# A two-layer perceiver kernel: products of the weights' low 64 rows in pairs on the two halves of the array

## The chip, the core and the metric

The kernel runs on one core of one Trainium2 chip. The metric is the device time of one execution in microseconds (us). A core has five engines with queues of their own: TensorE (PE in the profile; its weight loads are PEld), VectorE (DVE), ScalarE (ACT), GpSimd (POOL) and SyncE (SP), which issues the DMAs. They meet only at semaphores: a wait at the head of an engine's queue holds back all that stands behind it.

## What is computed

Six blocks are added to a residual `x` of 128 tokens x 256. The change touches two, the cross attentions over a context of 12544 rows x 192:

```python
x = x + _L0_xattn_ref(_layernorm(x), ctx_768, ...)   # 16 heads of 16
...
x = x + _L1_xattn_ref(_layernorm(x), ctx_768, ...)   # 16 heads of 64
# in each:
q = x @ Wq;  k = context @ Wk;  v = context @ Wv      # context 12544 x 192
sim = jnp.einsum('bhid,bhjd->bhij', q, k) * SCALE
attn = jax.nn.softmax(sim, axis=-1)
out = jnp.einsum('bhij,bhjd->bhid', attn, v)
```

Between and behind them stand a self attention, two mixtures of eight experts and one more attention over `x` itself; nothing in them is changed.

## The kernel before

Precision beyond float16 comes from splitting: a number is kept as a float16 (hi) and the float16 of what is left (low), and a product is summed from several float16 products in PSUM. The 192 rows of the context's transpose do not fit the 128 rows of the array. The first 128 lie in `ctxT_a_hi` and `ctxT_a_lo`. The last 64 lie in `ctxT_b`: its partitions 0 to 63 hold their hi part, 64 to 127 their low part. The weights stand in four parts, `wk16` and `wv16`: part 0 (first 128 rows, hi), part 1 (first 128 rows, low), part 2 (last 64 rows, hi, twice, so that one product covers hi x hi and low x hi) and part 3 (last 64 rows, low; its upper 64 partitions are zero). A key or value sum is therefore five products, all with 128 rows; in the fifth half of the rows are zeros.

The context has 98 tiles of 128 tokens (NT), in 14 chunks (NCH) of 7 tiles (CH, 896 columns). Each cross attention has two passes.

- The first pass (`first_pass`, L761) works by a list of turns written out beforehand, `TURNS`. PE transposes the chunks (layer 0 alone; `turn_ab` L697, `turn_lo` L709), makes key blocks of 128 rows x 896 columns in two PSUM banks of 448 (`project_keys` L715), and multiplies them with the queries (`score_pair` L749) to find each query's maximum. `score_pair` works with 64 rows: its two heads stand in the two halves of the array. ACT copies a block's hi part out (`keys_out` L1078, recorded at L1090 or L1088), DVE takes the low part (`keys_low_out` L1282, recorded at L1261 or L1291), and SP stores both to DRAM. Half of the maxima are reduced by DVE (L1324), the others copied by ACT (L1102) and merged by DVE (`merge`, L1261). Layer 0 has 28 blocks, layer 1 has 112. Layer 0's values are also made there (`values0` L740).
- The second pass of layer 1 (`attend1` L870) runs over two halves `g` of 8 heads, each over 98 tiles. PE's order in an iteration `t` is: five products for the values of tile `t` (`value_products` L733, 512 columns each), 16 score products (`score1` L835), and 16 products that weigh the values of tile `t - 1` (`weigh1` L853). ACT (L1143) takes the exponential of each group of four heads twice, once as float16 and once in place, and in odd tiles copies the values' hi part (L1156) ahead of that. DVE (L1407) first makes the values of tile `t` (`split_values1` L1362: in even tiles a cast, L1369, and a subtraction; in odd tiles only the subtraction), and then the low parts of the two groups of probabilities (L1261). The values have two PSUM banks in turn (`v_bank` L352), so the products of tile `i` wait until the values of `i - 2` are made (`values_made`, L879). Keys come back chunk by chunk (`load_keys1` L451), which may start once the chunk two before has been scored.

Nearly all matmuls are recorded at L679, a helper; they are told apart by their tiles.

Of the kernel before, what the change touches and what calls it, by code (L numbers as in the profile page):

```python
# [7 lines left out]
F32 = mybir.dt.float32  # L8
# [5 lines left out]
P = 128  # L14
# [27 lines left out]
def perceiver_kernel(nc, d, out):  # L42
# [18 lines left out]
    with ExitStack() as ctx:  # L61
# [39 lines left out]
        minus_half = sb("minus_half", [P, 1], F32)  # L101
        ps = ctx.enter_context(nc.psum_tensor("ps", [P, 8, 512], F32))
        col_in = att[:, 0:P]
        bk_scaled = small[:, 234:236]
# [67 lines left out]
        L0.wq, L0.wk, L0.wv = W[:, 0:512], W[:, 512:1024], W[:, 1024:1536]  # L172
        L0.wk16 = wv16[:, :, 256:512]
        L0.running = W[:, 5568:9152].bitcast(F16).rearrange("p (h k) -> p h k", h=H // 2)
        L0.k_parts = [W[:, 9152 + 448 * n:9152 + 448 * (n + 1)].bitcast(F16) for n in range(6)]
# [25 lines left out]
        QUERIES = (1, 2)  # L201
        W1_OFF, W2_OFF, CA_OFF = 7616, 8640, 9664

        def wview(off, a, b):
# [355 lines left out]
        def gpsimd(pool):  # L560
# [6 lines left out]

            def split_weights16(w, dst, n):
                top, rest = w[:, 0:n], w[0:CB, n:2 * n]
                settle(pool.tensor_scalar(top, top, VS, None, ALU.mult))  # L570
                settle(pool.tensor_copy(dst[:, 0, :], top))
                settle(pool.tensor_tensor(dst[:, 1, :], top, dst[:, 0, :], ALU.subtract))
                settle(pool.tensor_scalar(rest, rest, VS, None, ALU.mult))
                settle(pool.tensor_copy(dst[0:CB, 2, :], rest))
                settle(pool.tensor_tensor(dst[0:CB, 3, :], rest, dst[0:CB, 2, :], ALU.subtract))
                return pool.tensor_copy(dst[CB:P, 2, :], rest)

# [15 lines left out]
            pool.wait_ge(constants, 1)  # L593
            pool.memset(wv16[CB:P, 3, :].bitcast(F32), 0.0).then_inc(rows_blank, 1)
            pool.wait_ge(rows_blank, 1)
# [5 lines left out]
            pool.wait_ge(ld_w, PROJ_IN[0])  # L601
            split_weights16(L0.wk, L0.wk16, 256).then_inc(wk_made, 1)
            pool.wait_ge(wk_made, 1)
# [16 lines left out]
            pool.wait_ge(ld_wv, WV_IN[0])  # L620
            settle(split_weights16(L0.wv, wv16[:, :, 0:256], 256))
            settle(pool.memset(v_out[:, 0:VROW], 0.0))
# [19 lines left out]
            pool.wait_ge(step_pe, PE_B2)  # L642
            settle(pool.memset(L1.wk16[CB:P, 3, :].bitcast(F32), 0.0))
            pool.memset(q_two[CB:P, :].bitcast(F32), 0.0).then_inc(rows_blank, 1)
# [18 lines left out]
            pool.wait_ge(ld_wv, WV_IN[1])  # L663
            settle(split_weights16(L1.wv, wv16[:, :, 0:1024], 1024))
            for n in range(2):
# [11 lines left out]
        def tensor(pe):  # L677
# [19 lines left out]
            def turn_ab(c, slot):  # L697
                c16 = ctx16[c % 4]
                hi, b = (ps[:, 2 * slot + n, :].bitcast(F16) for n in range(2))
                pe.wait_ge(ctx_split, c + 1)  # L700
                for t in range(CH):
                    pe.transpose(hi[:, t * P:(t + 1) * P], c16[:, t, 0:P], ident16[:, :])
                for t in range(CH):
                    s = slice(t * P, (t + 1) * P)
                    pe.transpose(b[0:CB, s], c16[:, t, P:C], ident16[:, :])
                    ins = pe.transpose(b[CB:P, s], c16[:, t, C + P:2 * C], ident16[:, :])
                ins.then_inc(ab_turned, 1)
# [7 lines left out]
            def project_keys(L, b, slot):  # L715
                c, i = b // L.nI, b % L.nI
                ws = slice(i * P, (i + 1) * P)
                pe.wait_ge(wk_made, L.n + 1)
                if L is L0 and i == 0:
                    pe.wait_ge(hi_out, c + 1)  # L720
                    pe.wait_ge(b_out, c + 1)
                    pe.wait_ge(lo_out, c + 1)
                for n in range(MAXB):
                    ks = slice(c * CLEN + n * MAXC, c * CLEN + (n + 1) * MAXC)
                    o = ps[:, 2 * slot + n, 0:MAXC]
                    mm(o, L.wk16[:, 0, ws], ctxT_a_hi[:, ks], True, False)
                    mm(o, L.wk16[:, 1, ws], ctxT_a_hi[:, ks], False, False)
                    mm(o, L.wk16[:, 0, ws], ctxT_a_lo[:, ks], False, False)
                    mm(o, L.wk16[:, 2, ws], ctxT_b[:, ks], False, False)
                    ins = mm(o, L.wk16[:, 3, ws], ctxT_b[:, ks], False, True)  # L730
                ins.then_inc(keys_summed, 1)

            def value_products(o, ks, vs):  # L733
                mm(o, ctxT_a_hi[:, ks], wv16[:, 0, vs], True, False)
                mm(o, ctxT_a_hi[:, ks], wv16[:, 1, vs], False, False)
                mm(o, ctxT_a_lo[:, ks], wv16[:, 0, vs], False, False)
                mm(o, ctxT_b[:, ks], wv16[:, 2, vs], False, False)
                return mm(o, ctxT_b[:, ks], wv16[:, 3, vs], False, True)

            def values0(c, u, slot):  # L740
                pe.wait_ge(wv_made, 1)
                a, b = VPARTS[u]
                for t in range(a, b):
                    k = c * CH + t
                    ins = value_products(ps[:, 2 * slot, (t - a) * L0.gw:(t - a + 1) * L0.gw],
                                         slice(k * P, (k + 1) * P), slice(0, L0.gw))
                ins.then_inc(values0_summed, 1)
# [87 lines left out]
            def score1(g, t, j):  # L835
                i, n = (g * NT + t) * 2 + j, g * NCH + t // CH
                if i >= 3:
                    pe.wait_ge(low_made, i - 2)
                if t % CH == 0 and j == 0:
                    pe.wait_ge(ld_keys[n % 2], 48 * (NCH // 2) + 48 * (n // 2 + 1))  # L840
                    if n == 1:
                        pe.wait_ge(keys_const, 3)
                own = slice(t % CH * P, (t % CH + 1) * P)
                both, hi = KW1[n % 2]
                for k in range(4):
                    hh = 4 * j + k
                    qs = slice((8 * g + hh) * P, (8 * g + hh + 1) * P)
                    o = s_bank(i)[:, k * P:(k + 1) * P]
                    mm(o, both[:, hh, own], q_one[:, qs], True, False)
                    ins = mm(o, hi[:, hh, own], q_two[:, qs], False, True)  # L850
                ins.then_inc(scored, 1)

            def weigh1(g, t):  # L853
# [14 lines left out]
                ins.then_inc(weighed, 1)  # L868

            def attend1():  # L870
                first_pass(L1)
                pe.wait_ge(wv_made, 2)
                pe.wait_ge(keys_const, 2)
                for g in range(2):
                    for t in range(NT + 1):
                        if t < NT:
                            i = g * NT + t
                            if i >= 2:
                                pe.wait_ge(values_made, i - 1)  # L879
                            value_products(v_bank(i), slice(t * P, (t + 1) * P),  # L880
                                           slice(g * L1.gw, (g + 1) * L1.gw)).then_inc(values_summed, 1)
                            if g == 0 and t == 0:
                                pe.wait_ge(q_placed, 2)
                                pe.wait_ge(rows_made, 2)
                            for j in range(2):
                                score1(g, t, j)
                        if t:
                            weigh1(g, t - 1)
# [174 lines left out]
        def scalar(act):  # L1063
# [14 lines left out]
            def keys_out(L, b, slot):  # L1078
                n = L.k0 + b
                src = ps[:, 2 * slot:2 * slot + 2, 0:MAXC]  # L1080
                dst = k_part(L, b, 0).rearrange("p (n k) -> p n k", n=MAXB)
                act.wait_ge(keys_summed, n + 1)
# [169 lines left out]
        def vector(dve):  # L1252
# [29 lines left out]
            def keys_low_out(L, b, slot):  # L1282
                n = L.k0 + b
                src = ps[:, 2 * slot:2 * slot + 2, 0:MAXC]
                hi, low = (k_part(L, b, part).rearrange("p (n k) -> p n k", n=MAXB) for part in range(2))
                dve.wait_ge(keys_hi, n + 1)
# [226 lines left out]
            for e in range(NE):  # L1513
# [8 lines left out]
                                     op0=ALU.mult, op1=ALU.subtract)  # L1522
            dve.scalar_tensor_tensor(out=L1.wk16[0:CB, 3, :], in0=wk_b, scalar=VS, in1=L1.wk16[0:CB, 2, :],
                                     op0=ALU.mult, op1=ALU.subtract).then_inc(wk_made, 1)
            dve.wait_ge(q_hi, 4)
# [76 lines left out]
```

## Time and profile before

| | us |
|---|---|
| median of three runs (1548.43 to 1552.89) | 1550.3 |
| the profiled execution | 1556.26 |
| its span, first to last instruction | 1554.5 |

| engine | busy us | share of the span |
|---|---|---|
| PE | 1396.2 | 90% |
| PEld | 925.5 | 60% |
| DVE | 1055.4 | 68% |
| ACT | 1062.3 | 68% |
| POOL | 89.9 | 6% |

The chain that ended last is 60% PE and 21% DVE, 11% is issue and 4% DMA. The stages, by the profile's slices: layer 0's first pass until about 280 us, its second pass to 488, the small blocks and layer 0's experts to 613, layer 1's first pass from 622 to about 909, its second pass from about 919 to 1477, the rest to the end. A busy share says how full an engine was, not whether the others waited for it; ends of matmuls are modelled, so the distance between two starts is the safer number.

### The profile page before, as it was taken

The page shows a single profiled execution, that of the slowest core. Times are in us where ns is not written, and L with a number is a line of the kernel's source. Part 1 is how long each engine was busy: PE and PEld are TensorE (multiplying, and loading weights), DVE is VectorE, ACT ScalarE, POOL GpSimd, SP SyncE. Part 2 cuts the span into 40 slices and gives each one's busy share as a digit, 9 for nine tenths or more (in the row PEclk, how much of TensorE's full clock was granted, in tenths as well). Part 3 has the DMA queues.
Part 4 walks back from the last instruction along what each step waited for, and adds up shares of the span by engine and source line. Part 5 has one row for each costly group of instructions (what it writes and reads, how often), then busy time and mean ns, then how long its engine had stood idle before and what let it go on. Part 6 is the DMA issues. An engine that isn't in the chain of part 4 may idle for free.

```text
span 1554.5 us, 36882 instructions
## 1 busy us (share of the span) xinstructions
PE 1396.2 (90%) x15312; PEld 925.5 (60%) x15312; DVE 1055.4 (68%) x1480; ACT 1062.3 (68%) x1628; POOL 89.9 (6%) x85
## 2 busy tenths in 40 slices
PE   4888888799998789999999959999998999989959
PEld 2334444576775578343443427777776777767748
DVE  4899999200001311899999978888888888878832
ACT  3677777698995023666666648888887888878810
POOL 5311111000000001400000000000000000000000
PEclk9999999999998689999999979999999999999969
DMA  4245433775765134554454487777777677796620
GB/s 133 107 143 211 150 120 141 197 175 142 177 158 191 54 112 153 207 185 183 178 187 181 180 194 138 149 147 148 149 139 140 118 148 148 149 259 117 175 98 4
DMA packets 128458, 236.47 MB, mean 152 GB/s; under 512 B 8908, under 2 KB 113830, under 8 KB 128294
## 3 DMA queue, kind: packets, MB, share of 16 engines
q1 hardware_dynamic: 128294, 234.13, 57.0%
q8 instruction: 122, 2.00, 0.6%
q14 instruction: 42, 0.34, 0.1%
HBM read 155.98 MB, written 78.12 MB: 151 GB/s over the span
## 4 chain that ended last, share of the span: by engine, by line
PE 60%; DVE 21%; issue 11%; DMA 4%; ACT 2%; SPq 2%; POOL 0%; POOLq 0%; DVEq 0%; ACTq 0%
PE ps L679 59%; DVE W L1261 6%; DVE p L1261 5%; DVE small L1324 5%; DMA W<-keys_hi 2%; SPq L402 1%; DMA W<-in_ctx_dram 1%; ACT W L1088 1%; DVE W L1291 1%; DVE q_all L1261 1%; SPq L460 0%; ACT p L1102 0%; DVE ctxT_a_lo L1317 0%; DMA att<-in_L_ffn_b_dram 0%; DVE ctxT_b L1313 0%
## 5 line engine op out<-in xcount | busy, mean ns | idle before, releaser
L1261 DVE TENSOR_TENSOR p<-ps,p 128x512 f16<-128x512 f32 (+1 forms) x467 | 353.0, 756 | 76.5 <-ACT ps L1065 74.1
L1065 ACT ACTIVATE p<-ps 128x512 f16<-128x512 f32 (+1 forms) x490 | 329.3, 682 | 99.3 <-PE ps L679 97.0
L679 PE MATMUL ps<-q_all,W 128*128 128x128 f16 (+2 forms) x3544 | 264.3, 227 | 15.6 <-DMA W<-keys_hi 11.0
L679 PEld LDWEIGHTS ps<-q_all,W 128*128 128x128 f16 (+1 forms) x3544 | 230.8, 99 | 77.2 <-issue 25.5
L1324 DVE TENSOR_REDUCE small<-ps 128x1 f32<-128x896 f32 x224 | 245.3, 1096 | 6.1 <-PE ps L679 5.8
L1065 ACT ACTIVATE ps<-ps 128x512 f32<-128x512 f32 x392 | 236.0, 602 | 0.0
L679 PE MATMUL ps<-v,p 128*128 128x130 f16 x3136 | 170.4, 207 | 5.4 <-DVE p L1261 3.8
L679 PE MATMUL ps<-wv,ctxT_a_hi 128*128 128x512 f16 (+1 forms) x588 | 156.3, 347 | 13.6 <-DVE W L1291 6.1
L679 PE MATMUL ps<-wv,ctxT_b 128*128 128x512 f16 (+1 forms) x588 | 155.5, 346 | 0.0
L679 PEld LDWEIGHTS ps<-v,p 128*128 128x128 f16 x3136 | 148.4, 98 | 11.7 <-ACT ps L1065 4.0
L1261 DVE TENSOR_TENSOR v<-ps,v 128x512 f16<-128x512 f32 x196 | 135.5, 691 | 17.4 <-ACT v L1156 4.9
L1377 DVE COPY att<-ps 128x512 f32<-128x512 f32 x1 | 0.7, 690 | 207.5 <-PE ps L679 207.5
L679 PE MATMUL ps<-W,q_all 64*128 64x448 f16 (+1 forms) x684 | 105.7, 365 | 29.2 <-DVE ctxT_a_lo L1317 9.4
L679 PE MATMUL ps<-ctxT_a_hi,q_all 128*128 128x448 f16 (+1 forms) x464 | 126.3, 356 | 0.6 <-DVE p L1261 0.6
L679 PE MATMUL ps<-ctxT_b,q_all 128*128 128x448 f16 (+1 forms) x464 | 125.1, 353 | 0.0
L1090 ACT CAST p<-ps 128x896 f16<-128x896 f32 x75 | 67.9, 905 | 61.0 <-PE ps L679 60.9
L1102 ACT CAST p<-ps 128x896 f16<-128x896 f32 x104 | 92.8, 906 | 18.4 <-PE ps L679 17.6
L679 PE MATMUL ps<-wv,ctxT_a_lo 128*128 128x512 f16 (+1 forms) x294 | 102.0, 347 | 0.0
L1065 ACT ACTIVATE W<-ps 128x1024 f32<-128x1024 f32 x98 | 95.0, 1021 | 8.6 <-PE ps L679 6.4
L679 PEld LDWEIGHTS ps<-wv,ctxT_b 128*128 128x128 f16 x588 | 57.9, 99 | 49.7 <-issue 2.2
L679 PEld LDWEIGHTS ps<-W,q_all 64*128 64x128 f16 (+1 forms) x684 | 35.7, 108 | 81.9 <-issue 38.8
L679 PE MATMUL ps<-ctxT_a_lo,q_all 128*128 128x448 f16 (+1 forms) x240 | 82.7, 354 | 0.0
(223 smaller groups left out, 1753.5 us busy)
## 6 DMA issues: line engine op xcount, KB each, us to landing
W<-keys_hi SPq DMA_DIRECT2D x56, 896.0 KB, 14.7
W<-keys_low SPq DMA_DIRECT2D x28, 896.0 KB, 11.7
keys_hi<-p SPq DMA_DIRECT2D x75, 224.0 KB, 2.0
keys_low<-p SPq DMA_DIRECT2D x75, 224.0 KB, 1.9
keys_hi<-W SPq DMA_DIRECT2D x65, 224.0 KB, 2.0
keys_low<-W SPq DMA_DIRECT2D x65, 224.0 KB, 1.9
W<-values SPq DMA_DIRECT2D x14, 960.0 KB, 9.2
W<-in_L_ffn_W_dram SPq DMA_DIRECT2D x10, 1024.0 KB, 8.9
```

The lines of the kernel that those rows point to most:

```text
L402: sp.dma_start(by_rows(region, a, n), src.rearrange("(a p) n -> p a n", p=P)).then_inc(s, 16)
L679: return pe.matmul(out_, lhsT, rhs, start=start, stop=stop, **kw)
L1065: return act.activation(out_, in_, ACT.Exp, scale=scale)
L1088: ins = act.activation(dst, src, ACT.Identity, bias=bk_scaled[:, i:i + 1])
L1090: ins = act.copy(dst, src)
L1102: act.copy(dst.rearrange("p (n k) -> p n k", n=MAXB), src).then_inc(max_copied, 1)
L1261: return dve.tensor_tensor(out_, a, b, op)
L1291: ins = dve.scalar_tensor_tensor(out=low, in0=src, scalar=bk_scaled[:, i:i + 1], in1=hi, op0=ALU.add, op1=ALU.subtract)
L1324: dve.tensor_reduce(mpart[:, among(L, h), n:n + 1], ps[:, 2 * pair:2 * pair + 2, 0:MAXC], AX.XY, ALU.max).then_inc(max_reduced, 1)
L1377: dve.tensor_copy(att[:, 512:1024], ps[:, O0_BANK, :]).then_inc(outT_made, 1)
```

## The change

Part 3 of the weights (the low part of the last 64 rows) is written to both halves of the partitions instead of one half and zeros. `ctxT_b` is laid out in two ways: `half_of(c, t)` says in which half of the partitions a tile's hi part lies; tiles 0 to 3 of a chunk differ from tiles 4 to 6, and even chunks from odd ones. So the fifth product can be made with 64 rows, in one half of the array or the other, by the tile.

```diff
+        FIRST = 4
+        def half_of(c, t):
+            return (t >= FIRST) ^ c % 2
+        def tile_at(i):
+            c, r = i // CH, i % CH
+            return c * CH + (r // 2 if r % 2 == 0 else FIRST + r // 2)
...  turn_ab
+                    k = half_of(c, t)
+                    pe.transpose(b[k * CB:(k + 1) * CB, s], c16[:, t, P:C], ident16[:, :])
+                    ins = pe.transpose(b[(1 - k) * CB:(2 - k) * CB, s], c16[:, t, C + P:2 * C], ident16[:, :])
...  project_keys: banks of 512 and 384 columns; four products each as before, then
+                for n, (k0, k1) in enumerate(banks):
+                    k = half_of(c, FIRST * n)
+                    rows = slice(k * CB, (k + 1) * CB)
+                    ins = mm(ps[:, 2 * slot + n, 0:k1 - k0], L.wk16[rows, 3, ws],
+                             ctxT_b[rows, c * CLEN + k0:c * CLEN + k1], False, True)
...  layer 1's values
+            def values1(i):
+                g, t = i // NT, tile_at(i % NT)
+                vs = slice(g * L1.gw, (g + 1) * L1.gw)
+                if i >= 2:
+                    pe.wait_ge(values_made, i - 1)
+                value_products(v_bank(i), slice(t * P, (t + 1) * P), vs)
+                if i % 2:
+                    for n, t in ((i - 1, tile_at(i % NT - 1)), (i, t)):
+                        k = half_of(t // CH, t % CH)
+                        rows = slice(k * CB, (k + 1) * CB)
+                        mm(v_bank(n), ctxT_b[rows, t * P:(t + 1) * P], wv16[rows, 3, vs], False, True).then_inc(values_summed, 1)
...  attend1, in iteration t
-                            if i >= 2:
-                                pe.wait_ge(values_made, i - 1)
-                            value_products(v_bank(i), slice(t * P, (t + 1) * P),
-                                           slice(g * L1.gw, (g + 1) * L1.gw)).then_inc(values_summed, 1)
+                            if t == 0:
+                                values1(i)
+                            if i + 1 < 2 * NT and t + 1 < NT:
+                                values1(i + 1)
```

`value_products` is now the first four products. In layer 1's second pass the tiles of a chunk are taken in the order 0, 4, 1, 5, 2, 6, 3 (`tile_at`), so that halves alternate; `score1` takes the same order. Layer 0's values keep five products of 128 rows: their part 3 exists in two forms, with the zeros below or above, and the tile chooses. The keys' copies out of PSUM read 896 columns in one run instead of 2 x 448. POOL's `split_weights16` ends with one more copy of 64 rows; for layer 1's keys DVE makes part 3 in two instructions (L1523), and POOL's memset of its zeros (L643) goes.

## Rows read from the trace of the kernel before

**Rows 1.** Three stretches: busy us of PE, PEld, DVE, ACT, POOL, then clock, DMA.

```profile
120.00:200.00 80.00, 63.98 (x534) 33.21 (x532) 76.83 (x91) 58.29 (x73) 13.76 (x5) 1.00 0.47 169
760.00:800.00 40.00, 40.00 (x224) 15.89 (x222) 40.00 (x49) 26.94 (x33) 0.00 (x0) 1.00 0.49 180
1000.00:1100.00 100.00, 99.83 (x1369) 77.10 (x1367) 85.58 (x130) 85.90 (x167) 0.00 (x0) 1.00 0.75 145
```

**Rows 2.** Timeline, layer 1's first pass: start, duration, engine, line, out<-in, count [idle].

```profile
761.61 1.11 DVE L1324 TENSOR_REDUCE small<-ps 128x1 f32<-128x896 f32 x1
762.61 1.11 DVE L1261 TENSOR_TENSOR p<-ps,p 128x896 f16<-128x896 f32 x1
763.61 0.64 DVE L1261 TENSOR_TENSOR W<-W,att 128x896 f16<-128x896 f16 x1
763.77 0.11 PEld L679 LDWEIGHTS ps<-ctxT_a_hi,q_all 128*128 128x128 f16 x2 [0.42 <-DVE p L1261]
764.14 1.11 DVE L1324 TENSOR_REDUCE small<-ps 128x1 f32<-128x896 f32 x1
```

**Rows 3.** Timeline, the same pass in its first chunk, PE alone.

```profile
629.28 0.54 PE L679 MATMUL ps<-ctxT_b,q_all 128*128 128x448 f16 x2
629.75 0.55 PE L679 MATMUL ps<-W,q_all 64*128 64x448 f16 x4
630.24 0.55 PE L679 MATMUL ps<-ctxT_a_hi,q_all 128*128 128x448 f16 x2
...
632.72 0.55 PE L679 MATMUL ps<-ctxT_a_hi,q_all 128*128 128x448 f16 x2
```

**Rows 4.** Timeline, layer 0's first pass, VectorE.

```profile
188.64 0.61 DVE L1261 TENSOR_TENSOR W<-W,p 128x896 f16<-128x896 f16 x1
189.39 1.15 DVE L1291 SCALAR_TENSOR_TENSOR W<-ps,small,W 128x896 f16<-128x896 f32 x1
```

**Rows 5.** Timeline, layer 1's second pass, two tiles: even from 1061.54, odd from 1064.29.

```profile
1061.54 0.59 PE L679 MATMUL ps<-wv,ctxT_a_hi 128*128 128x512 f16 x2
1061.97 0.38 PE L679 MATMUL ps<-wv,ctxT_a_lo 128*128 128x512 f16 x1
...
1062.62 1.06 PE L679 MATMUL ps<-q_all,W 128*128 128x128 f16 x16
...
1063.26 0.60 ACT L1065 ACTIVATE p<-ps 128x512 f16<-128x512 f32 x1 [0.54 <-PE ps L679]
...
1064.29 0.59 PE L679 MATMUL ps<-wv,ctxT_a_hi 128*128 128x512 f16 x2
...
1065.37 1.06 PE L679 MATMUL ps<-q_all,W 128*128 128x128 f16 x16
1065.57 0.59 ACT L1156 CAST v<-ps 128x512 f16<-128x512 f32 x1 [0.21 <-PE ps L679]
1066.05 0.60 ACT L1065 ACTIVATE p<-ps 128x512 f16<-128x512 f32 x1
...
1066.95 0.59 PE L679 MATMUL ps<-wv,ctxT_a_hi 128*128 128x512 f16 x2
...
1068.17 0.69 DVE L1261 TENSOR_TENSOR p<-ps,p 128x512 f16<-128x512 f32 x1 [0.30 <-ACT ps L1065]
...
1068.78 0.68 DVE L1369 CAST v<-ps 128x512 f16<-128x512 f32 x1
...
1069.49 0.69 DVE L1261 TENSOR_TENSOR v<-ps,v 128x512 f16<-128x512 f32 x1
```

**Rows 6.** Waits of PE from 925 to 1485: total us, times, longest.

```profile
PE ps L679 <- DMA W<-keys_hi: 11.0, 2, 6.0
...
PE ps L679 <- issue: 3.5, 6, 1.4
```

**Rows 7.** Timeline, where the low parts of the keys' weights are made.

```profile
23.18 0.39 POOL L576 CAST wv<-W 64x256 f16<-64x256 f32 x1
...
616.54 1.21 DVE L1523 SCALAR_TENSOR_TENSOR q_all<-stage,q_all 64x1024 f16<-64x1024 f32 x1
```

More of the change, by code:

```diff
@@ L102, in perceiver_kernel @@
         ps = ctx.enter_context(nc.psum_tensor("ps", [P, 8, 512], F32))
+        ps_row = ps[:, :, :].rearrange("p b n -> p (b n)")
         col_in = att[:, 0:P]
@@ L173, in perceiver_kernel @@
         L0.wk16 = wv16[:, :, 256:512]
+        L0.wv_low = wv16[:, 3, 0:256], wv16[:, 3, 512:768]
         L0.running = W[:, 5568:9152].bitcast(F16).rearrange("p (h k) -> p h k", h=H // 2)
@@ L566, in rsqrt_var, with split_weights16 @@
                 pool.tensor_tensor(rstd, rstd, minus_half[:, :], ALU.pow).then_inc(ln_rstd, 1)
-            def split_weights16(w, dst, n):
+            def split_weights16(w, dst, n, low):
                 top, rest = w[:, 0:n], w[0:CB, n:2 * n]
@@ L575, in split_weights16 @@
                 settle(pool.tensor_tensor(dst[0:CB, 3, :], rest, dst[0:CB, 2, :], ALU.subtract))
-                return pool.tensor_copy(dst[CB:P, 2, :], rest)
+                pool.tensor_copy(dst[CB:P, 2, :], rest)
+                return pool.tensor_copy(low, dst[0:CB, 3, :])
             pool.memset(ident[:, :], 0.0)
@@ L593, in gpsimd @@
             pool.wait_ge(constants, 1)
-            pool.memset(wv16[CB:P, 3, :].bitcast(F32), 0.0).then_inc(rows_blank, 1)
+            pool.memset(wv16[CB:P, 3, 0:256].bitcast(F32), 0.0)
+            pool.memset(wv16[0:CB, 3, 512:768].bitcast(F32), 0.0).then_inc(rows_blank, 1)
             pool.wait_ge(rows_blank, 1)
@@ L601, in gpsimd @@
             pool.wait_ge(ld_w, PROJ_IN[0])
-            split_weights16(L0.wk, L0.wk16, 256).then_inc(wk_made, 1)
+            split_weights16(L0.wk, L0.wk16, 256, L0.wk16[CB:P, 3, :]).then_inc(wk_made, 1)
             pool.wait_ge(wk_made, 1)
@@ L620, in gpsimd @@
             pool.wait_ge(ld_wv, WV_IN[0])
-            settle(split_weights16(L0.wv, wv16[:, :, 0:256], 256))
+            settle(split_weights16(L0.wv, wv16[:, :, 0:256], 256, L0.wv_low[1][CB:P, :]))
             settle(pool.memset(v_out[:, 0:VROW], 0.0))
@@ L642, in gpsimd @@
             pool.wait_ge(step_pe, PE_B2)
-            settle(pool.memset(L1.wk16[CB:P, 3, :].bitcast(F32), 0.0))
             pool.memset(q_two[CB:P, :].bitcast(F32), 0.0).then_inc(rows_blank, 1)
@@ L663, in gpsimd @@
             pool.wait_ge(ld_wv, WV_IN[1])
-            settle(split_weights16(L1.wv, wv16[:, :, 0:1024], 1024))
+            settle(split_weights16(L1.wv, wv16[:, :, 0:1024], 1024, wv16[CB:P, 3, 0:1024]))
             for n in range(2):
@@ L704, in turn_ab @@
                     s = slice(t * P, (t + 1) * P)
-                    pe.transpose(b[0:CB, s], c16[:, t, P:C], ident16[:, :])
-                    ins = pe.transpose(b[CB:P, s], c16[:, t, C + P:2 * C], ident16[:, :])
+                    k = half_of(c, t)
+                    pe.transpose(b[k * CB:(k + 1) * CB, s], c16[:, t, P:C], ident16[:, :])
+                    ins = pe.transpose(b[(1 - k) * CB:(2 - k) * CB, s], c16[:, t, C + P:2 * C], ident16[:, :])
                 ins.then_inc(ab_turned, 1)
@@ L722, in project_keys @@
                     pe.wait_ge(lo_out, c + 1)
-                for n in range(MAXB):
-                    ks = slice(c * CLEN + n * MAXC, c * CLEN + (n + 1) * MAXC)
-                    o = ps[:, 2 * slot + n, 0:MAXC]
+                banks = ((0, FIRST * P), (FIRST * P, CLEN))
+                for n, (k0, k1) in enumerate(banks):
+                    ks = slice(c * CLEN + k0, c * CLEN + k1)
+                    o = ps[:, 2 * slot + n, 0:k1 - k0]
                     mm(o, L.wk16[:, 0, ws], ctxT_a_hi[:, ks], True, False)
@@ L729, in project_keys @@
                     mm(o, L.wk16[:, 2, ws], ctxT_b[:, ks], False, False)
-                    ins = mm(o, L.wk16[:, 3, ws], ctxT_b[:, ks], False, True)
+                for n, (k0, k1) in enumerate(banks):
+                    k = half_of(c, FIRST * n)
+                    rows = slice(k * CB, (k + 1) * CB)
+                    ins = mm(ps[:, 2 * slot + n, 0:k1 - k0], L.wk16[rows, 3, ws],
+                             ctxT_b[rows, c * CLEN + k0:c * CLEN + k1], False, True)
                 ins.then_inc(keys_summed, 1)
@@ L737, in value_products @@
                 mm(o, ctxT_b[:, ks], wv16[:, 2, vs], False, False)
-                return mm(o, ctxT_b[:, ks], wv16[:, 3, vs], False, True)
             def values0(c, u, slot):
@@ L744, in values0 @@
                     k = c * CH + t
-                    ins = value_products(ps[:, 2 * slot, (t - a) * L0.gw:(t - a + 1) * L0.gw],
-                                         slice(k * P, (k + 1) * P), slice(0, L0.gw))
+                    o, ks = ps[:, 2 * slot, (t - a) * L0.gw:(t - a + 1) * L0.gw], slice(k * P, (k + 1) * P)
+                    value_products(o, ks, slice(0, L0.gw))
+                    ins = mm(o, ctxT_b[:, ks], L0.wv_low[half_of(c, t)], False, True)
                 ins.then_inc(values0_summed, 1)
@@ L842, in score1 @@
                         pe.wait_ge(keys_const, 3)
+                t = tile_at(t)
                 own = slice(t % CH * P, (t % CH + 1) * P)
@@ L1079, in keys_out @@
                 n = L.k0 + b
-                src = ps[:, 2 * slot:2 * slot + 2, 0:MAXC]
-                dst = k_part(L, b, 0).rearrange("p (n k) -> p n k", n=MAXB)
+                src, dst = ps_row[:, 1024 * slot:1024 * slot + CLEN], k_part(L, b, 0)
                 act.wait_ge(keys_summed, n + 1)
@@ L1283, in keys_low_out @@
                 n = L.k0 + b
-                src = ps[:, 2 * slot:2 * slot + 2, 0:MAXC]
-                hi, low = (k_part(L, b, part).rearrange("p (n k) -> p n k", n=MAXB) for part in range(2))
+                src = ps_row[:, 1024 * slot:1024 * slot + CLEN]
+                hi, low = (k_part(L, b, part) for part in range(2))
                 dve.wait_ge(keys_hi, n + 1)
@@ L1522, in vector @@
                                      op0=ALU.mult, op1=ALU.subtract)
-            dve.scalar_tensor_tensor(out=L1.wk16[0:CB, 3, :], in0=wk_b, scalar=VS, in1=L1.wk16[0:CB, 2, :],
-                                     op0=ALU.mult, op1=ALU.subtract).then_inc(wk_made, 1)
+            for k in range(2):
+                ins = dve.scalar_tensor_tensor(out=L1.wk16[k * CB:(k + 1) * CB, 3, :], in0=wk_b, scalar=VS,
+                                               in1=L1.wk16[0:CB, 2, :], op0=ALU.mult, op1=ALU.subtract)
+            ins.then_inc(wk_made, 1)
             dve.wait_ge(q_hi, 4)
```

## The prediction, made before the changed kernel was run

> **What bounds the kernel now.** I read the stretches of each stage first, then the timelines inside them. In both first passes VectorE is the full engine: 76.83 of 80 us in layer 0, 40.00 of 40 in layer 1, at full TensorE clock (1.00, the 2.4 GHz level) [rows 1]. Inside layer 1 the order is reduce, subtraction, merge, reduce, each starting as the one before drains: starts at 761.61, 762.61, 763.61, 764.14, so 2.53 us a block, all of it VectorE [rows 2]. In layer 1's second pass PE is the full engine (99.83 of 100 us, DVE 85.58, ACT 85.90) [rows 1]. There two tiles take 1066.95 - 1061.54 = 5.41 us of PE starts without a gap: five value products of 0.215 each (two in 1061.97 - 1061.54 = 0.43) make 1.08, scores and weighing 1.67 in the even tile and 1.58 in the odd [rows 5]. So only PE work of that last stage is on the path that sets the end, and of the change only what falls there can count in full.
>
> **The change, part by part.** The sum is made against the profiled execution, 1556.3 us, which is 6.0 above the median of 1550.3; I take the difference over to the median.
>
> *Keys.* A block loses two fifth products of 448 columns (2 x 0.19: 629.66 less 629.28 is the pace [rows 3]) and gains a pair in two halves that lasts as long as its longer one, 512 columns, 0.215. That is 0.16 us of PE per block. That such pairs overlap the trace shows: the four 64-row products of 448 columns start at 629.75 and the next product starts at 630.24, 0.49 later, where four in a row would take 0.76 [rows 3]. In layer 1, 104 of 112 blocks run at VectorE's 2.53 [rows 2]: gain 0. In its first chunk there is nothing to merge and PE sets the pace, 632.72 - 630.24 = 2.48 a block [rows 3], while VectorE has two operations of 1.0: 8 x 0.16 = -1.3. In layer 0 VectorE waits only for the block that follows its queue's merge: 189.39 - 188.64 = 0.75, where that step takes 0.53 elsewhere [rows 2, 4]. Of this 0.22, 0.16 goes, in some 13 chunks: -2. Bounds: 0 and 28 x 0.16 = -4.5.
>
> *Weights.* POOL's extra copy of 64 x 256 costs about 0.39 [rows 7] ahead of the first keys, of which the queries' placing hides most: I take +0.4. DVE's second L1523 (1.21 [rows 7]) lies beside the query projection of layer 1, for whose end both engines wait: 0. The other copies on POOL lie beside 250 us of first pass, and the transposes are as many as before: 0. If the cover of these were gone it would be +0.4, +1.2 and, for 64 x 1024 on POOL, a few us.
>
> *Layer 1's values, PE's side.* Per two tiles one product of 512 columns goes: -0.215, or -21 us over 98 pairs, if PE still sets the pace and nothing else is added.
>
> *Layer 1's values, the waits.* This is where I part from the plain sum. The even tile's last product is now issued with the odd tile's, at the same place in PE's order as before (1.08 us into the even iteration). But its successor's place has moved: the products of tile t + 2 now stand at the head of iteration t + 1, one whole iteration earlier, and they need the bank that tile t's split still reads (`values_made`). Before, the split had 5.41 - 1.08 = 4.3 us; now it has scores and weighing of one iteration, 1.67 us. It does not fit: it is a cast and a subtraction, and in VectorE's queue it stands behind the last low part of the tile before. The rows show it: low part at 1068.17, cast at 1068.78, subtraction at 1069.49 to 1070.18, while the even iteration began at 1066.95: the values are made 3.23 us into it, and the next iteration's products would want them after 2.6 to 2.75 [rows 5].
>
> That closes a loop, which I follow from the start of an odd iteration (four products, of the even tile to come):
> - four products 4 x 0.215 = 0.86;
> - scores start to first exponential: 1063.26 - 1062.62 = 0.64 (the even tile, where ScalarE was idle; the odd tile's copy, which held ScalarE up at 1065.57, can now go before the scores, as its values are summed an iteration earlier);
> - first exponential to the last low part of that tile: 1068.17 - 1066.05 = 2.12;
> - low part to cast 0.61, cast to subtraction 0.71, subtraction 0.69;
> - its end to PE's next weight load: 763.77 - (762.61 + 1.11) = 0.05 [rows 2].
>
> The sum is 5.68 (0.86 + 0.64 + 2.12 + 0.61 + 0.71 + 0.69 + 0.05), and with 0.01 for a cold start of the first product 5.69, against 5.41 now. PE's own work in the pair of tiles is 5.20, so it would stand for about 0.5 us before every even tile's products. Behind that wait stand the odd tile's scores, so ScalarE and VectorE come late too, which is why the loop doesn't close shorter. The odd tile's values (copy on ScalarE, subtraction) are made 1.9 us into the odd iteration and are wanted at 2.45: no wait. Per pair +0.28, 98 pairs: +27.4. At each half's start two tiles' products are issued ahead of the first scores, beside a wait, and the last iteration has none: -0.9 twice, -2 in all.
>
> *The keys' loads.* PE waits 11.0 us for keys in this stage, 6.0 of them at its start, and 3.5 for "issue", mostly at a new chunk's first scores [rows 6]. The loads run beside the tiles; a chunk of seven tiles will take 19.9 instead of 18.9 us, and the 5 us wait that remains comes two chunks after its loads may start. Back come 3 of the 3.5, and 2 of the 5: -5. Bounds: 0 and -8.5.
>
> *A rule on the array's modes.* Value products have 128 rows on both sides of the new pair. Before the change such a change of rows happens between keys and scores: the second 448-column product of [rows 3] ends at 629.66 and the 64-row ones start at 629.75; they last 0.38 and the next 128-row product starts at 630.24: 0.09 and 0.11 us beyond the streams. So a pair among the values costs about 0.2 on top, in the even iteration, where PE otherwise stands 0.5: the loop is unchanged, and my sum too. In the keys the number of changes stays two a block. The Trainium skill ("TensorEngine Tiling (Array Packing)", Tiling Modes, Key Properties) says that changing the tiling mode drains TensorE, and that speaks against this change: by it PE's side would gain nothing even without the new wait; without it PE's side would give -21.
>
> The sum: +27.4 - 2 - 5 - 2 - 1.3 + 0.4 = +17.5. Profiled 1573.8, median **1567.8 us**.
>
> **The rivals.**
> - *The wait is not late, and PE keeps the pace; changes of rows are free.* 98 x -0.215 = -21, -3.3 from the first passes, and about +4 as chunks of 18.2 us run into the keys' loads (three issue waits would each grow by 0.7, and more appear): 1530. For it: PE is at 99.83%. Against it: the loop would have to be 0.3 to 0.5 us shorter than rows of this very sequence.
> - *PE keeps the pace, and the changes of rows cost what rows 3 show.* -21 + 98 x 0.2 - 3 = -4: 1546 to 1550, no change to barely faster. It needs the same shorter loop, below 5.4.
> - *The pairs do not overlap.* Then the even iteration has 0.2 more, still under the 0.5 for which PE stands (with the changes of rows just under it), and the first passes give nothing: 1571. Against it: the 0.49 us for four in [rows 3].
> - *The clock.* PE stands still every 5.7 us; if that brought the granted clock to the 1.2 GHz level for stretches, each pair of tiles there would take some 4 us more, hundreds of us if all through. Against it: in layer 0's first pass PE is busy 63.98 of 80 us, in bits, and the clock is 1.00 [rows 1]; here it would be 91%.
>
> **How the numbers follow.** Forecast 0.80; no overlap 0.06; clock 0.02 (slower by far); PE keeps the pace with the costs of a row change 0.06 (half of it beyond the bound of faster), free 0.05; 0.01 left. About what can be told from no change is 0.3%, 4.7 us. The range: each 0.05 us in the loop is 5 us; with 0.1 either way it is -10 and +10; the loads add from +5 (nothing back) to -3.5, the first passes +3 to -2.5. Put together these give 1556 to 1580, which with the no-overlap case holds about 0.85. Faster 0.08, same 0.04, slower 0.88.
>
> **What would show it.** In layer 1's second pass: two tiles in 5.69 us; PE's waits before `ctxT_a_hi` products on `DVE v`, one in each two tiles, 0.3 to 0.5 us, 30 to 45 us in sum, or on PEld; low part, cast and subtraction back to back on VectorE; VectorE and ScalarE less busy than before. In layer 1's first pass still 2.53 us a block, with longer idle on PE. Layer 0's first pass 2 us shorter. Wrong it would be if two tiles take 5.4 or less: then the split's place in VectorE's queue or the exponentials' start is not as I put it. If they take 5.69 and the total is still below 1560, my loads' share was too small.

## The result

| | median us | against before, 95% interval |
|---|---|---|
| before | 1551.4 (4 runs) | |
| changed | 1574.96 (1573.3 to 1582.01, 4 runs) | 1.0163 [1.0127, 1.0199] |
| changed, once more | 1574.79 (6 runs; before 1552.23, 11 runs) | 1.0144 [1.0122, 1.0165] |

The change makes the kernel slower by 1.4% to 1.6%, 22 to 25 us. The forecast was 1567.8, slower, so the direction came true and the size was 5 to 7 us too small. The profiled execution of the changed kernel took 1573.87 us with a span of 1572.1, 17.6 above the profiled one of before, which was 5 us above its own median.

### The profile page after: what moved, and what is told of

It reads as the page before. It is cut to its first block, busy times and chain, and to the rows that moved or that the text cites. A ratio compares the mean times of both kernels' runs of the same rounds, so it can differ in the third digit from the quotient of the medians.

```text
span 1572.1 us, 36886 instructions
## 1 busy us (share of the span) xinstructions
PE 1381.3 (88%) x15312; PEld 899.4 (57%) x15312; DVE 1047.6 (67%) x1481; ACT 1064.6 (68%) x1628; POOL 90.8 (6%) x88
## 4 chain that ended last, share of the span: by engine, by line
PE 38%; DVE 25%; issue 20%; ACT 9%; DMA 4%; SPq 2%; POOL 0%; POOLq 0%; DVEq 0%; ACTq 0%
PE ps L695 37%; ACT ps L1101 6%; DVE p L1296 5%; DVE W L1296 5%; DVE small L1359 4%; DVE v L1296 4%; DVE v L1404 4%; DMA W<-keys_hi 2%; SPq L417 1%; DMA W<-in_ctx_dram 1%; ACT W L1123 1%; DVE W L1326 1%; ACT p L1101 1%; DVE q_all L1296 1%; DMA keys_hi<-p 0%
## 5 line engine op out<-in xcount | busy, mean ns | idle before, releaser
L695 PEld LDWEIGHTS ps<-q_all,W 128*128 128x128 f16 (+1 forms) x3544 | 222.9, 99 | 69.5 <-issue 41.7
L1359 DVE TENSOR_REDUCE small<-ps 128x1 f32<-128x896 f32 x224 | 241.7, 1080 | 4.1 <-PE ps L695 3.8
L695 PE MATMUL ps<-wv,ctxT_b 128*128 128x256 f16 (+2 forms) x588 | 144.7, 349 | 0.0
L695 PE MATMUL ps<-ctxT_a_hi,q_all 128*128 128x512 f16 (+1 forms) x464 | 126.3, 356 | 15.2 <-DVE p L1296 0.6
L695 PE MATMUL ps<-ctxT_b,q_all 128*128 128x512 f16 (+1 forms) x464 | 118.5, 357 | 0.0
L695 PEld LDWEIGHTS ps<-ctxT_a_hi,q_all 128*128 128x128 f16 (+1 forms) x464 | 37.6, 101 | 89.8 <-DVE p L1296 41.9
L695 PEld LDWEIGHTS ps<-wv,ctxT_b 128*128 128x128 f16 (+1 forms) x588 | 48.0, 96 | 68.0 <-issue 43.1
L695 PE MATMUL ps<-ctxT_a_lo,q_all 128*128 128x512 f16 (+1 forms) x240 | 82.7, 354 | 0.0
```

The source lines that it names most:

```text
L695: return pe.matmul(out_, lhsT, rhs, start=start, stop=stop, **kw)
L1359: dve.tensor_reduce(mpart[:, among(L, h), n:n + 1], ps[:, 2 * pair:2 * pair + 2, 0:MAXC], AX.XY, ALU.max).then_inc(max_reduced, 1)
```

## The profile after

First the same three stretches as in [rows 1]. In layer 1's first pass VectorE is full as before and PE falls from 40.00 to 37.65; in the second pass PE falls from 99.83 to 96.42, VectorE from 85.58 to 79.55 and ScalarE from 85.90 to 82.38, at the same full clock. All three are less busy in the second pass, as they are when each waits for another in turn.

```profile
120.00:200.00 80.00, 63.24 (x524) 32.55 (x526) 77.83 (x93) 59.65 (x76) 13.67 (x5) 1.00 0.44 158
760.00:800.00 40.00, 37.65 (x223) 15.13 (x222) 40.00 (x48) 26.91 (x33) 0.00 (x0) 1.00 0.50 184
1000.00:1100.00 100.00, 96.42 (x1297) 70.17 (x1296) 79.55 (x123) 82.38 (x160) 0.00 (x0) 1.00 0.73 139
```

Next the timeline of two tiles of the changed kernel's second pass, the answer to [rows 5]. The even iteration begins at 1059.85, the odd one at 1063.10, the next even one at 1065.56: 5.71 us for two tiles (1065.56 - 1059.85), against 5.41.

```profile
1059.85 0.59 PE L695 MATMUL ps<-wv,ctxT_a_hi 128*128 128x512 f16 x2
...
1060.50 0.70 PE L695 MATMUL ps<-wv,ctxT_b 128*128 128x512 f16 x3
1060.81 0.10 PEld L695 LDWEIGHTS ps<-wv,ctxT_b 64*128 64x128 f16 x2 [0.42 <-issue]
...
1061.03 0.69 DVE L1296 TENSOR_TENSOR p<-ps,p 128x512 f16<-128x512 f32 x1 [0.31 <-ACT ps L1101]
...
1061.13 1.07 PE L695 MATMUL ps<-q_all,W 128*128 128x128 f16 x16
1061.63 0.68 DVE L1404 CAST v<-ps 128x512 f16<-128x512 f32 x1
...
1062.35 0.69 DVE L1296 TENSOR_TENSOR v<-ps,v 128x512 f16<-128x512 f32 x1
...
1063.09 0.11 PEld L695 LDWEIGHTS ps<-wv,ctxT_a_hi 128*128 128x128 f16 x2 [0.35 <-DVE v L1296]
1063.10 0.60 PE L695 MATMUL ps<-wv,ctxT_a_hi 128*128 128x512 f16 x2 [0.20 <-DVE v L1296]
...
1063.97 1.06 PE L695 MATMUL ps<-q_all,W 128*128 128x128 f16 x16
...
1064.62 0.60 ACT L1101 ACTIVATE p<-ps 128x512 f16<-128x512 f32 x1 [0.23 <-PE ps L695]
...
1065.56 0.59 PE L695 MATMUL ps<-wv,ctxT_a_hi 128*128 128x512 f16 x2
...
1066.74 0.69 DVE L1296 TENSOR_TENSOR p<-ps,p 128x512 f16<-128x512 f32 x1 [0.31 <-ACT ps L1101]
```

On VectorE the low part (1061.03), the cast (1061.63) and the subtraction (1062.35 to 1063.04) stand behind each other; PE's next weight load starts at 1063.09, 0.05 after it, behind the wait. From PE's start at 1063.10: scores after 0.87, exponential after 0.65, low part after 2.12, and around again.

The chain of waits over such a stretch (start, duration, what) runs through just these links; in the kernel before, the same view of this stage named only PE.

```profile
1063.10 1.50 PE ps L695 x12
...
1065.11 0.59 ACT ps L1101
...
1066.10 0.61 ACT ps L1101
...
1066.74 0.04 DVE p L1296
...
1067.34 0.69 DVE v L1404
1068.06 0.70 DVE v L1296
1068.76 0.05 issue
1068.81 1.50 PE ps L695 x12
```

PE's waits in this stage (columns as in [rows 6], but from 915 to 1500, since the stage begins 7 us earlier here): the new one comes 86 times in the matmuls' record. The loads of keys cost 7.8 instead of 11.0, the issue waits 4.7 instead of 3.5.

```profile
PEld ps L695 <- DVE v L1296: 32.5, 89, 2.1
PE ps L695 <- DVE v L1296: 19.0, 86, 1.9
PE ps L695 <- DMA W<-keys_hi: 7.8, 2, 4.3
...
PE ps L695 <- issue: 4.7, 3, 3.2
```

Last the first pass of layer 1, for [rows 2] and [rows 3]. With merges the reduces are 762.04 - 759.51 = 2.53 us apart as before, and only the weight loads' idle before the next block grew, from 0.42 to 0.59. In the first chunk two blocks' first products are 626.32 - 624.00 = 2.32 us apart, where it was 2.48.

```profile
624.00 0.60 PE L695 MATMUL ps<-ctxT_a_hi,q_all 128*128 128x512 f16 x2
...
626.32 0.60 PE L695 MATMUL ps<-ctxT_a_hi,q_all 128*128 128x512 f16 x2
...
759.11 0.11 PEld L695 LDWEIGHTS ps<-ctxT_a_hi,q_all 128*128 128x128 f16 x2 [0.59 <-DVE W L1296]
...
759.51 1.08 DVE L1359 TENSOR_REDUCE small<-ps 128x1 f32<-128x896 f32 x1
...
762.04 1.08 DVE L1359 TENSOR_REDUCE small<-ps 128x1 f32<-128x896 f32 x1
```

## The experiments

Theory A is the forecast's: the values' products of the next tile stand an iteration earlier, their wait for `values_made` closes a loop through the scores, ScalarE and VectorE, and that costs 0.29 us for two tiles. Its main rival B: the pairs' changes of rows cost PE that time. Rival C: the tile order, the layout or the banks of 512 and 384 columns. Below, "two tiles" is the most frequent distance between the casts of a tile's values and of those two tiles on, in layer 1's second pass.

**The place alone.** The kernel before, with the products one tile ahead:

```diff
-                            if i >= 2:
-                                pe.wait_ge(values_made, i - 1)
-                            value_products(v_bank(i), ...)
+                            for n in ((i, i + 1) if t == 0 else (i + 1,) if t + 1 < NT else ()):
+                                if n >= 2:
+                                    pe.wait_ge(values_made, n - 1)
+                                value_products(v_bank(n), ...)
```

> Edit: the kernel before, with the five full products of tile t+1 at the head of iteration t, and nothing else of the change. Theory A: the same loop, with five products in it instead of four: 1.08 + 0.64 + 2.12 + 0.61 + 0.71 + 0.69 + 0.05 = 5.90 us per two tiles, +0.48 x 98 = +47 less 5 to 8 of keys' waits that come back: 1588 to 1598, slower than the changed kernel. Rival B: no row changes, so the time of before, 1551. Rival C (order of tiles and layout): 1551 too.

Measured: 1588.63 us, ratio 1.0247 [1.0218, 1.0275], two tiles in 5.92 to 5.93. Nothing of the pairs, the layout or the tile order is in this kernel, and it is slower than the changed one. B and C fall as causes; the loop with five products is 0.215 longer than with four, as its sum says. The wait, on PE (1100.11 begins the even iteration, 1103.35 the odd one, 1106.03 the next even one; the wait is at the odd one, as in the changed kernel):

```profile
1100.11 0.59 PE L679 MATMUL ps<-wv,ctxT_a_hi 128*128 128x512 f16 x2
...
1103.35 0.61 PE L679 MATMUL ps<-wv,ctxT_a_hi 128*128 128x512 f16 x2 [0.37 <-DVE v L1262]
...
1106.03 0.59 PE L679 MATMUL ps<-wv,ctxT_a_hi 128*128 128x512 f16 x2
```

**The keys alone.** The changed kernel, but layer 1's values as before:

```diff
+                g, t = i // NT, i % NT          # natural order, in score1 too
+                mm(v_bank(i), ctxT_b[:, t * P:(t + 1) * P], wv16[:, 3, vs], False, True).then_inc(values_summed, 1)
...  attend1: values1(i) at the head of iteration t, nothing ahead
```

> Edit: the changed kernel's keys, layout and first passes, but layer 1's values as before: five products of 128 rows of tile t at the head of iteration t, tiles in natural order (part 3 of the weights stays in both halves of the partitions, so the fifth product adds the low x low term too). Theory A: second pass at 5.42 per two tiles, first passes 3 to 7 us shorter: 1544 to 1549. Rival C (layout or banks of 512 and 384 cost something): above 1551.

> The keys-only version (changed keys and layout, values as before) once more beside the next kernel: 1546 to 1551, 5.42 us per two tiles in layer 1's second pass.

Measured: 1548.52 us, ratio 0.9988 [0.9971, 1.0005], two tiles in 5.41 to 5.42; the second time 1550.66 us, 0.9988 [0.9970, 1.0006]. So the rest of the change costs nothing that can be told from no change: the medians lie 2.3 and 1.3 us below the kernel before, and both intervals include a ratio of 1. Both times are inside their ranges.

**Two full products in the pair's place.**

```diff
-                        mm(v_bank(n), ctxT_b[rows, ...], wv16[rows, 3, vs], False, True).then_inc(values_summed, 1)
+                        mm(v_bank(n), ctxT_b[:, ...], wv16[:, 3, vs], False, True).then_inc(values_summed, 1)
```

> Edit: the changed kernel with two 128-row products in the place of the pair of 64-row ones, nothing else moved. The pair takes 0.63 with its full product before it, i.e. 0.41 for itself; two full ones take 0.43. Theory A: same loop, 5.70 us per two tiles, 1572 to 1578, and PE's even iteration is as long as with the pair. Rival B: without changes of rows it is up to 0.2 x 98 = 20 us faster, 1555.

Measured: 1577.12 us, ratio 1.0173 [1.0145, 1.0201], two tiles in 5.71. No row changes, and the same time within the noise: they are not in the loop. So the pair is worth nothing that shows where it stands.

**A row change by itself.** The keys-only kernel with the fifth product by 64 rows, alone:

```diff
-                mm(v_bank(i), ctxT_b[:, ...], wv16[:, 3, vs], False, True)...
+                k = half_of(t // CH, t % CH)
+                rows = slice(k * CB, (k + 1) * CB)
+                mm(v_bank(i), ctxT_b[rows, ...], wv16[rows, 3, vs], False, True)...
```

> Edit: keys-only version (five products of tile t at the head of iteration t, natural order) with the fifth product made by 64 rows in one half of the array, alone in its tile: two changes of rows for each tile, no pair, no earlier place of the values. It prices a change of rows on PE by itself. Theory A: PE sets the pace there, 5.42 + 4 x 0.10 = 5.82 us per two tiles and 0.41 from the 64-row product's start to the scores' plus the change before it; +39 over the keys-only version: 1583 to 1592. If changes of rows were free: 5.42 and 1548.

Measured: 1578.5 us, ratio 1.0166 [1.0141, 1.0191], two tiles in 5.75 to 5.76: 28 to 30 us over the keys-only kernel, and below the range I gave (1583 to 1592). The price itself is as stated: five products take 1060.06 - 1058.78 = 1.28 us here and 1061.96 - 1060.88 = 1.08 in the keys-only kernel, so a pair of changes is 0.20. But the distance between two such iterations grew only to 1061.66 - 1058.78 = 2.88, twice of which is 5.76, not 5.82: PE had up to 0.09 of idle for two tiles in the kernel before that I had counted as work (more below). First this kernel, then keys-only:

```profile
1058.78 0.59 PE L695 MATMUL ps<-wv,ctxT_a_hi 128*128 128x512 f16 x2
...
1060.06 1.07 PE L695 MATMUL ps<-q_all,W 128*128 128x128 f16 x16
...
1061.66 0.59 PE L695 MATMUL ps<-wv,ctxT_a_hi 128*128 128x512 f16 x2
```

```profile
1060.88 0.59 PE L695 MATMUL ps<-wv,ctxT_a_hi 128*128 128x512 f16 x2
...
1061.96 1.06 PE L695 MATMUL ps<-q_all,W 128*128 128x128 f16 x16
1062.94 0.86 PE L695 MATMUL ps<-v,p 128*128 128x130 f16 x16
```

**The wait moved behind the scores.**

```diff
-                            if i + 1 < 2 * NT and t + 1 < NT:
-                                values1(i + 1)
                             for j in range(2):
                                 score1(g, t, j)
+                            if i + 1 < 2 * NT and t + 1 < NT:
+                                values1(i + 1)
```

> Edit: the changed kernel, but the products of tile t+1 stand behind the scores of tile t instead of ahead of them (pairs, row changes, tile order and keys all kept). Theory A (the values' wait closes a loop of 5.7 us per two tiles): the wait has 0.9 us more, PE sets the pace again, 1.28 + 0.86 + 1.67 + 1.58 = 5.39 to 5.42 us per two tiles, total 1545 to 1552. Rival B (the loss is the pairs' changes of rows on PE): nothing moves, 5.7 us and about 1575.

Measured: 1631.25 us, ratio 1.0519 [1.0494, 1.0544], two tiles in 6.36 to 6.37. Both expectations missed. I had looked at one wait only. The even tile is now summed 0.9 us later, its split starts later, and in VectorE's queue the low parts of the same tile stand behind the split (cast at 1101.62 after 1.82 of idle, low parts from 1102.96, though the first group's exponentials had ended at 1101.08). The odd tile's second group of scores needs the bank that the first of these frees:

```profile
1100.49 0.59 ACT L1101 ACTIVATE ps<-ps 128x512 f32<-128x512 f32 x1
...
1101.62 0.69 DVE L1404 CAST v<-ps 128x512 f16<-128x512 f32 x1 [1.82 <-PE ps L695]
...
1102.96 1.28 DVE L1296 TENSOR_TENSOR p<-ps,p 128x512 f16<-128x512 f32 x2
...
1103.70 0.62 PE L695 MATMUL ps<-q_all,W 128*128 128x128 f16 x8 [0.86 <-DVE p L1296]
```

A pair needs both tiles' products before either split may start, so with two PSUM banks for the values I see only a late split or a bank asked for early. No run tried a third place, or a third bank.

**A link taken out of the loop.** The changed kernel, with the even tile's cast moved from VectorE to ScalarE:

```diff
-                        if i % 2:
-                            act.wait_ge(values_summed, i + 1)
+                        act.wait_ge(values_summed, i + 1)     # copy in every tile, VectorE only subtracts
```

> Edit: the changed kernel, but ScalarE makes the values' hi part in even tiles too (copy ahead of the tile's exponentials); VectorE only subtracts. Pairs, places and order are kept. Theory A: the loop loses VectorE's cast (0.71) behind the low part; what then binds is the even tile's sum 1.28, start 0.18, copy 0.5, exponentials 2.09, low part 0.03 + 0.69, 0.05, weighing 0.70 = 5.52 us per two tiles: 1551 to 1559. Rival B (the pair's changes of rows): no gain, 1575.

Measured: 1567.69 us, ratio 1.0105 [1.008, 1.013], two tiles in 5.58 to 5.59. The loop gave way by 0.12 and another took over, the one that I named, but 0.07 us longer, and the total is 9 us above my range. Its links (even iteration from 1101.57): values 1.28, copy 0.10 later, exponential 0.56 after the copy, 2.12 to the low part at 1105.63, 0.69, and 0.15 until the weighing starts at 1106.47, where I had 0.05 for the last; with 0.70 of weighing it makes 5.60. Over 98 pairs the 0.07 makes 7 us of the miss; the other 2 were not followed up. Against the changed kernel this is 7 us less, where rival B had said no gain.

```profile
1101.57 0.59 PE L695 MATMUL ps<-wv,ctxT_a_hi 128*128 128x512 f16 x2
...
1102.85 1.07 PE L695 MATMUL ps<-q_all,W 128*128 128x128 f16 x16
1102.95 0.59 ACT L1190 CAST v<-ps 128x512 f16<-128x512 f32 x1 [0.45 <-PE ps L695]
1103.51 0.60 ACT L1101 ACTIVATE p<-ps 128x512 f16<-128x512 f32 x1
...
1105.63 0.69 DVE L1295 TENSOR_TENSOR p<-ps,p 128x512 f16<-128x512 f32 x1 [0.31 <-ACT ps L1101]
...
1106.47 0.74 PE L695 MATMUL ps<-v,p 128*128 128x130 f16 x13
```

**What bounds the kernel before.** That idle asked for an answer. In [rows 5] the even tile's scores and weighing take 1.67, the odd's 1.58. If the 5.42 of before is a loop as well, it runs through ScalarE's copy in odd tiles. The keys-only kernel with that copy on VectorE:

```diff
-                        if i % 2:
-                            act.wait_ge(values_summed, i + 1)
-                            ...                               # ScalarE's copy is gone
+                dve.wait_ge(values_summed, i + 1)             # VectorE casts in every tile
```

> Edit: the keys-only version, with VectorE casting the values of odd tiles too; ScalarE's copy (L1156) ahead of the odd tiles' exponentials goes. Theory D (the 5.42 us of the kernel before is itself a loop: odd tile's values 1.08, copy begins 0.20 later, exponentials 0.48 after it, 2.12 to the last low part, 0.69, 0.15 to the weighing's start, 0.70 weighing = 5.42, in which PE stands 0.09 ahead of every odd tile's weighing): the copy's detour goes, the start of the exponentials is 0.64 behind the scores' (1.72 instead of 1.76), 5.38 us per two tiles, -4 us: 1543 to 1547. Rival (PE's work alone is 5.42): 5.42 and no change. A third outcome, should VectorE's fourth cast or subtraction come late: above 5.42.

Measured: 1547.98 us (12 runs; before 1551.99, 23 runs), ratio 0.9971 [0.9955, 0.9988], two tiles in 2.67 + 2.71 = 5.38. That is the distance that the theory gave; the time is 1 us above its range. The version is faster than the kernel before, by 4.0 us of median, and it holds the keys in pairs and none of the change's values. How much of this the copy gives is less sure: against the keys-only kernel beside it the median is 2.7 us lower, which is about the noise of the two, and in the traces the stage is 1.2 and 1.9 us shorter than in the two keys-only ones (547.6 against 548.8 and 549.5), not 4.

```profile
1099.95 0.59 PE L695 MATMUL ps<-wv,ctxT_a_hi 128*128 128x512 f16 x2
...
1102.66 0.59 PE L695 MATMUL ps<-wv,ctxT_a_hi 128*128 128x512 f16 x2
...
1105.33 0.59 PE L695 MATMUL ps<-wv,ctxT_a_hi 128*128 128x512 f16 x2
```

**The changed kernel once more.**

> The changed kernel once more, for a narrower figure. Theory A, from the profiled spans of both (+17.6 us) and the stages of their traces (second pass of layer 1 +24, first passes -3 to -7): 1568 to 1576, with 5.71 us per two tiles again.

Measured: 1574.79 us, two tiles in 5.71, inside the range.

## Why the prediction was right, point by point

- *The loop.* Forecast 5.69 us for two tiles, measured 5.71, through the links as listed. The wait was forecast at 0.3 to 0.5 us, 30 to 45 in sum, and is 0.35 and 32.5 on PEld. That the place of the products does it, and not the pairs, is shown by the place-alone kernel (5.92) and by the one with full products (5.71).
- *The size in this stage.* Forecast +20.4 (27.4 less 2 at the ends less 5 for loads). From the first exponential to the last tile's normalising it was 1476.99 - 926.02 = 551.0 before and 1494.23 - 918.99 = 575.2 after: +24.3, and +23.0 in the second profile. The loop alone is 98 x 0.30 = 29. So ends and loads gave back 5, not 7: PE's waits for keys fell by 3.2, but the issue waits did not fall. This part varies from one execution to another: in the kernel with two full products, with the same 5.71, the stage took 569.1. The bounds of the stage, first before, then after:

```profile
926.02 0.60 ACT L1065 ACTIVATE p<-ps 128x512 f16<-128x512 f32 x1 [15.96 <-PE ps L679]
...
1476.99 0.35 DVE L1396 COPY att<-ps 128x192 f32<-128x192 f32 x1
```

```profile
918.99 0.60 ACT L1101 ACTIVATE p<-ps 128x512 f16<-128x512 f32 x1 [16.08 <-PE ps L695]
...
1494.23 0.34 DVE L1431 COPY att<-ps 128x192 f32<-128x192 f32 x1
```

- *Row changes.* Forecast 0.2 for a pair of them, hidden in PE's wait: 0.20 measured, hidden. In the changed kernel a full product, the pair and two changes take 1061.13 - 1060.50 = 0.63, i.e. 0.215 + 0.215 + 0.20. In the single-half kernel a full product and one 64-row product alone take 1060.06 - 1059.43 = 0.63 too, so the second of a pair costs nothing: the pair overlaps, and the gain of one product is just what the row changes cost. The Trainium skill ("TensorEngine Tiling (Array Packing)", Tiling Modes, Key Properties) says that changing the tiling mode drains the engine. The runs agree that such a change costs time, 0.10 us each; whether a drain is behind it, no row says.
- *Layer 1's first pass.* Forecast -1.3, from the first chunk: the pass took 298.6 us before (616.02 to 914.63) and 297.5 after (609.95 to 907.49), -1.1. The other trace with the first passes of before has 298.7, the other eight with the changed ones 297.3 to 297.9.
- *Layer 0's first pass.* Forecast -2. Its chunks came every 17.72 us before and every 17.67 after, -0.7 over 13; the rest by which this stage ended earlier (277.5 to 273.6) is not the change's, since that end lay between 273.6 and 276.9 in the other ten traces, at 275.3 in the place-alone kernel, which has the first passes of before. Of the 0.22 us on VectorE only 0.06 went (the step takes 203.45 - 202.76 = 0.69 after); why not 0.16 was not followed up.
- *Weights.* Forecast +0.4. No run shows it: VectorE's first low part of keys begins at 28.67 before, and between 28.20 and 29.50 in the nine traces with the change's weights.
- *What was wrong beside it.* The step "two tiles take 5.41 us of PE starts without a gap" is wrong by 0.09: ends of matmuls are modelled, and a wait of that size does not show as idle. PE's own work is 5.33 (5.42 less the 0.09 by which the even tile's scores and weighing outlast the odd's), and the kernel before was already held by a loop; the kernel with VectorE's casts, at 5.38, is the evidence. It left the forecast whole, but the two rivals in which "PE keeps the pace" rested on it.

The sum by measured terms: +24, -1.1, -0.7, that is +22, against +17.5 forecast and 22 to 25 measured. That the profiled execution, 1573.87, hits the 1573.8 of the forecast is luck: the changed kernel's layer 1 pass began 6.1 us earlier than before (616.02 to 609.95), and it lay between 609.4 and 614.9 in the other nine traces, so most of that is not the change's.

## What to carry to other kernels

Issuing work earlier on a full engine is not free when it asks for a buffer that a consumer still reads: count the time from the last write of the buffer to its next request, and set it against the consumer's place in its own queue. Then follow every wait around to where it began; a sum along such a loop, with durations and start distances from one timeline, gave the period to 0.02 us here, and to 0.07 where a link's price was taken from another wait. The experiment that moved the wait elsewhere was judged by one wait alone and was off by 80 us.

## What the runs showed of the hardware that was not expected

- Between 128-row and 64-row products of 512 columns a change costs PE 0.10 us, half of the 0.20 measured for going and coming back; the weight loads stand idle for 0.42 before the 64-row one. One fifth product in 64 rows alone is thus a loss of 0.20, a pair a gain of 0.01 to 0.02 (0.63 against three full products, 0.645).
- After VectorE's end the first product that waited for it starts 0.06 us later where it is the values' (1063.04 to 1063.10), and 0.15 later where it is the weighing's (1106.32 to 1106.47). What makes the difference was not tested.
- The granted clock stays at its full level, 2.4 GHz, under such a loop: 1.00 from 1000 to 1100 us, with PE at 96.42 of 100, and 0.99 over the stage (925 to 1475), as before.
